# One prologue folded into the attention part: one input norm, inputs rounded tile by tile, a first step that begins with the context

## The chip, the cores and the metric

The kernel runs on one NeuronCore of a Trainium2 chip. The metric is the device time of one execution in microseconds. The engines are TensorE (PE: matmuls, with PEld its weight loads), VectorE (DVE), ScalarE (ACT), GpSimd (POOL) and SyncE (SP), which issues most DMAs. They run beside each other and wait for one another on semaphores.

## What is computed

A gated transformer block with cross attention and a mixture of experts on `x` of 8 sequences of 112 tokens and 512 channels. Cut to what matters here:

```
h   = layernorm(layernorm(x)) * ln_w + ln_b                 # two norms in a row, eps 1e-5
xq_n = fp8(bf16(clip(h / in_scale_n, -448, 448)))           # n = q, qx, k, v: four roundings
q, qx, k, v = xq_n @ (wq, wqx, wk, wv)                      # then a layernorm per head of 128
kx, vx      = split(ctx @ w_kv_x)                           # ctx of 375 rows, not rounded
core, xout  = attention(q, k, v), attention(qx, kx, vx)     # 16 heads, 8 groups
x = x + tanh(g_x) * (fp8(concat(core, xout) / smooth) @ wproj) * scale
x = x + tanh(g_f) * experts(layernorm(x))                   # 8 experts, 2 of them per token
```

Two norms in a row are one: with mean m and variance v of a token, the second norm of the first is (x - m) / sqrt(v(1 + e) + e*e).

## The kernel before

Three parts stand behind each other, each with its own block of instruction streams, and a barrier between them.

`quantise_inputs` is the prologue. The 896 tokens are 7 tiles of 128. VectorE takes the statistics of a tile, GpSimd makes root and shift (L303, L305), ScalarE applies them (L314), and this twice for every tile, the second norm three tiles behind the first. TensorE transposes (L347), ScalarE applies `ln_w` and `ln_b` into `hT` (L320) and makes, for each of the four input scales, a bf16 copy of all 4 x 896 columns (L330). VectorE rounds each copy to fp8 in five operations of 3584 columns (`round_fp8`, L410 to L414) into `xq`. Between these copies ScalarE centres the first group's weights (`centre`, L149 to L154: 128 columns at a time are scaled, and the mean of the head's columns, made by VectorE at L130, is added).

`attention` does the heads in 4 groups (`gp`), each with its own 2048 columns of weights, and in a group a step per sequence (8). A matmul in f32 is done as three products of split operands: `w_hi` and `w_lo` are the high and low part of the weights, `c_hi` and `c_lo` of the context. ScalarE writes the high parts, VectorE or GpSimd the low ones. `xqs` is the tile of `xq` converted for the matmul (`inputs`, L1049). In a step `project(s, j)` makes six products: j = 0, 1, 2 from tokens (queries, cross queries, keys and values), j = 3, 4, 5 from the three thirds of the context. Steps 0 to 6 of a group have a token tile; step 7 has none left and only the rest. While step s is projected, step t = s - 1 has its scores, softmax and outputs: TensorE's, VectorE's and ScalarE's orders are written out by hand in `step`. The very first step (change = "first") has no t beside it. It needs all of `xq`, all `w_hi` and `w_lo`, and does j = 0 to 5 in that order.

In the first four steps with a tile behind the first one VectorE also takes the means of the next group's weights (`weights.means`), and ScalarE centres them one step later.

`projected_experts` follows and isn't touched.

The numbers `pj_no` and `st_no` give the count that the semaphores of projections and statistics have reached at product j of a step.

Of the kernel before, what the change touches and what calls it, by code (L numbers as in the profile page):

```python
# [19 lines left out]
U16 = mybir.dt.uint16  # L20
# [40 lines left out]
def transformer_block(nc, x, ctxT, vecs, scalars, smooth, w_in, wproj, Wr, Wg, Wu, Wd, out):  # L61
# [3 lines left out]
    with ExitStack() as top:  # L65
# [24 lines left out]
        with ExitStack() as c:  # L90
            xq = sb(c, "xq", [P, 4, KB, NT], BF16)
            smi = sb(c, "smi", [P, GP, 8])
            wsc = sb(c, "wsc", [P, 4, KB])
            wmul = sb(c, "wmul", [P, KB, LNC // HD])
            weights = CentredWeights(c, sb, sem, w_in, shared, wsc, wmul)
            with ExitStack() as c0:
                quantise_inputs(nc, c0, sb, ps, sem, x, vecs, scalars, smooth, vec, scal, gate,
                                proj_scale, ident, mhalf, epst, xq, smi, weights)
            with ExitStack() as c1:
                attention(nc, c1, sb, ps, sem, ctxT, wproj, cat_w, vec, ident, mhalf, epst, xq, smi,  # L100
                          weights, shared, wp_load, cat_load, results)
# [5 lines left out]
class CentredWeights:  # L107
# [3 lines left out]
    def __init__(self, c, sb, sem, w_in, shared, wsc, wmul):  # L111
# [3 lines left out]
        self.in_done = sem(c, "w_in_done")  # L115
# [5 lines left out]
    def fetch(self, sp, g, k):  # L121
        sp.dma_start(self.raw[:, k, :], self.w_in[g, :, k, :]).then_inc(self.in_done, 16)

    def means(self, v, g, k):

        mean = self.mean[:, bass.ds(k, 1), :].rearrange("p a b -> p (a b)")
        v.wait_ge(self.in_done, 16 * KB * (g + 1))
# [103 lines left out]
def quantise_inputs(nc, c, sb, ps, sem, x, vecs, scalars, smooth, vec, scal, gate, proj_scale,  # L231
                    ident, mhalf, epst, xq, smi, weights):

    LAG = 3
    NORMS = []
    for j in range(TJ + LAG):
        if j < TJ:  # L240
            NORMS.append((0, j))
        if j >= LAG:
            NORMS.append((1, j - LAG))
    N = len(NORMS)
    wsc, wmul = weights.wsc, weights.wmul

    xs = sb(c, "xs", [P, TJ, D])
    st = sb(c, "st", [P, N, 6])
    mv = sb(c, "mv", [P, N, 2])
    rstd = sb(c, "rstd", [P, N])  # L250
    shift = sb(c, "shift0", [P, N])
    hT = sb(c, "hT", [P, KB, NT])
    inv = sb(c, "inv", [P, 4, KB])
    smr = sb(c, "smr", [P, GP, 8])
    yq = sb(c, "yq", [P, 2, KB, NT], BF16)
    ye = sb(c, "ye", [P, KB, NT], BF16)
    ysum = sb(c, "ysum", [P, KB, NT], BF16)
    pt = ps(c, "pt", [P, 4, 512])

    vec_in = sem(c, "vec_in")  # L260
    x_in = [sem(c, f"x_in{j}") for j in range(TJ)]
    const_done = sem(c, "const_done")
    pool_self = sem(c, "pool_self")
    bn_done = sem(c, "bn_done0")
    ag_done = sem(c, "ag_done0")
    stat_done = sem(c, "stat_done")
    rstd_pow = sem(c, "rstd_pow0")
    rstd_done = sem(c, "rstd_done")
    normed = sem(c, "normed")
    dve = sem(c, "dve_chain0")  # L270
    tr_done = sem(c, "tr_done")
    hT_done = sem(c, "hT_done")
    scal_done = sem(c, "scal_done")
    inv_done = sem(c, "inv_done")
    y_done = sem(c, "y_done")
    round_done = sem(c, "round_done")
    block = c.enter_context(nc.Block())

    @block.sync
    def _(sp):  # L280
        tokens = x.rearrange("b t d -> (b t) d")
        sp.dma_start(xs[:, 0, :], tokens[0:P, :]).then_inc(x_in[0], 16)
        sp.dma_start(vec[:, :], vecs).then_inc(vec_in, 16)
        sp.dma_start(scal[:, :], scalars.partition_broadcast(P)).then_inc(vec_in, 16)
        sp.dma_start(smr[:, :, :], smooth).then_inc(vec_in, 16)
        for j in range(1, TJ):
# [1680 lines left out]
```

## Time and profile before

| | us |
|---|---|
| median of three timed runs (1179.20 to 1185.28) | 1180.48 |
| the profiled execution | 1179.41 |
| its span | 1177.6 |
| TensorE busy | 1081.8 (92%) |
| VectorE busy | 808.2 (69%) |
| ScalarE busy | 726.1 (62%) |
| GpSimd busy | 500.3 (42%) |
| mean granted TensorE clock | 0.967 of full speed |

Shares are means over stages that differ: the prologue, the attention and the experts. What a change in one stage is worth is read from that stage. Busy shares of TensorE count pipelined matmuls and are no measure of its peak.

### The profile page before, as it was taken

How to read it: one execution, taken by the hardware profiler on the slowest of the kernel's cores; microseconds unless marked ns; L12 is line 12 of the kernel's file. 1: busy time of each engine (PE TensorE's matmuls, PEld its weight loads, DVE VectorE, ACT ScalarE, POOL GpSimd, SP SyncE). 2: the span in 40 equal slices, each digit the busy share in tenths (PEclk: the TensorE clock that was granted, in tenths of full speed). 3: DMA queues.
4: the chain of work that ended last, by engine and by line, in shares of the span. 5: the costliest groups of instructions: out<-in, count | busy, mean ns of one | idle time of the engine just before them, and what ended most of it. 6: DMA issues, size and time to landing. Idle time of an engine off the chain costs nothing. (4 is left out here: it accounts for less than half of the span.)

```text
span 1177.6 us, 19559 instructions
## 1 busy us (share of the span) xinstructions
PE 1081.8 (92%) x5662; PEld 890.0 (76%) x5662; DVE 808.2 (69%) x1626; ACT 726.1 (62%) x2082; POOL 500.3 (42%) x587
## 2 busy tenths in 40 slices
PE   1079999999999999999999999998999959999996
PEld 1058888878888887888878888886888747777885
DVE  7967887797878787878789677767545776565000
ACT  7967887865788876687875676565231323333442
POOL 3065454445454544554545445542000125565432
PEclk9589999999999999999999999999999969999999
DMA  5032111115111113211111411110955237674220
GB/s 206 0 135 104 43 44 35 36 60 186 35 51 44 44 35 137 101 44 35 51 52 36 140 52 37 42 43 10 342 187 194 104 129 217 193 228 120 49 45 0
DMA packets 51714, 107.38 MB, mean 91 GB/s; under 512 B 5984, under 2 KB 26464, under 8 KB 49568
## 3 DMA queue, kind: packets, MB, share of 16 engines
q1 hardware_dynamic: 46912, 97.00, 25.2%
q0 software_dynamic: 4704, 9.18, 3.4%
q8 instruction: 49, 0.80, 0.3%
q14 instruction: 49, 0.40, 0.1%
HBM read 91.48 MB, written 16.52 MB: 92 GB/s over the span
## 5 line engine op out<-in xcount | busy, mean ns | idle before, releaser
L632 POOL TENSOR_TENSOR rs<-va,mhalf 125x2 f32<-125x2 f32 (+1 forms) x180 | 201.3, 1118 | 14.1
L638 POOL TENSOR_TENSOR c_lo<-c_raw,c_hi 128x500 fp32r<-128x500 f32 x96 | 122.8, 1279 | 183.3 <-ACT c_hi L689 183.3
L848 PE MATMUL p_proj<-w_hi,xqs 128*128 128x512 f32 (+2 forms) x464 | 157.0, 358 | 42.8 <-DVE w_lo L567 41.0
L875 PE MATMUL p_proj<-w_hi,c_hi 128*125 128x512 f32 x384 | 165.4, 431 | 0.0
L875 PE MATMUL p_proj<-w_hi,c_lo 128*125 128x512 f32 x384 | 151.5, 395 | 0.0
L875 PE MATMUL p_proj<-w_lo,c_hi 128*125 128x512 f32 x384 | 151.3, 394 | 0.0
L848 PE MATMUL p_proj<-w_lo,xqs 128*128 128x512 f32 (+2 forms) x464 | 147.9, 339 | 0.0
L848 PEld LDWEIGHTS p_proj<-w_hi,xqs 128*128 128x128 f32 (+1 forms) x464 | 86.4, 186 | 51.4 <-issue 43.5
L625 POOL TENSOR_TENSOR va<-ss,epst 125x2 f32<-125x2 f32 (+1 forms) x180 | 47.2, 262 | 170.7 <-DVE ss L1057 101.1
L767 ACT ACTIVATE pcross<-p_cross,nmax 112x375 f32<-112x375 f32 x128 | 73.6, 585 | 43.5 <-DVE nmax L1086 43.4
L919 PE MATMUL p_cross<-kxT,qxT 128*112 128x375 f32 x256 | 97.0, 480 | 0.0
L848 PEld LDWEIGHTS p_proj<-w_lo,xqs 128*128 128x128 f32 (+1 forms) x464 | 86.7, 187 | 8.3
L875 PEld LDWEIGHTS p_proj<-w_hi,c_hi 128*125 128x125 f32 x384 | 71.3, 186 | 18.4 <-issue 0.2
L875 PEld LDWEIGHTS p_proj<-w_lo,c_hi 128*125 128x125 f32 x384 | 71.3, 186 | 17.9
L875 PEld LDWEIGHTS p_proj<-w_hi,c_lo 128*125 128x125 f32 x384 | 71.1, 185 | 18.0
L729 ACT ACTIVATE nkx<-p_proj 125x256 f32<-125x256 f32 x96 | 38.4, 400 | 63.5 <-PE p_proj L875 63.5
L950 PE MATMUL p_out<-pcrossT,valx 125*128 125x224 f32 x354 | 76.6, 352 | 0.0
L1093 DVE TENSOR_SCALAR pcross<-pcross,linv 112x375 f32<-112x375 f32 x128 | 72.0, 562 | 4.6
L1086 DVE TENSOR_REDUCE nmax<-p_cross 112x1 f32<-112x375 f32 x128 | 69.0, 543 | 2.9 <-PE p_cross L919 0.2
L1469 POOL DMA_INDIRECT out<-p_cat,of_row x21 | 45.9, 2186 | 57.9 <-ACT p_cat L1570 50.2
L950 PEld LDWEIGHTS p_out<-pcrossT,valx 125*128 125x128 f32 x354 | 66.8, 189 | 0.3
L933 PEld LDWEIGHTS p_tr<-ident,pcross 112*125 112x125 f32 x384 | 51.9, 188 | 17.7 <-issue 13.5
(268 smaller groups left out, 2857.1 us busy)
## 6 DMA issues: line engine op xcount, KB each, us to landing
c_raw<-in_ctxT SPq DMA_DIRECT2D x96, 250.0 KB, 2.6
shared<-in_w_in SPq DMA_DIRECT2D x16, 1024.0 KB, 8.9
shared<-in_wproj SPq DMA_DIRECT2D x32, 256.0 KB, 3.9
raw_g<-in_Wg SPq DMA_DIRECT2D x8, 1024.0 KB
raw_u<-in_Wu SPq DMA_DIRECT2D x8, 1024.0 KB, 6.2
raw_d<-in_Wd SPq DMA_DIRECT2D x8, 1024.0 KB, 5.5
cat_scratch<-results SPq DMA_DIRECT2D x32, 224.0 KB, 2.0
shared<-cat_scratch SPq DMA_DIRECT2D x2, 1792.0 KB, 9.2
```

Of the source, the lines that this page charges most:

```text
L625: pool.tensor_tensor(va[0:rows, lo:hi], ss[0:rows, lo:hi], epst[0:rows, lo:hi], ALU.add).then_inc(va_done, 1)
L632: pool.tensor_tensor(rs[0:rows, lo:hi], va[0:rows, lo:hi], mhalf[0:rows, lo:hi], ALU.pow).then_inc(rs_done, 1)
L638: pool.tensor_tensor(flat(c_lo[:, k, :, :]), flat(c_raw[:, k, :, :]), flat(c_hi[:, k, :, :]).bitcast(F32), ALU.subtract).then_inc(cl_done, 1)
L767: act.activation(pcross[0:T, h, :], p_cross[0:T, h % 2, 0:TC], ACT.Exp, bias=nmax[0:T, 4 + h:5 + h], accum_out=lsum[0:T, 4 + h:5 + h]).the ...
L848: m = pe.matmul(out, xqs[:, n, k, 0:rows], (w_hi, w_lo)[i % 2][:, k, lo:lo + w], start=(i == 0), stop=(i == 2 * KB - 1))
L875: m = pe.matmul(bank[0:CT, :], a[:, ch, k, :], w[:, k, CKX:CV], start=(i == 0), stop=(i == 3 * KB - 1))
L919: pe.matmul(p_cross[0:T, h % 2, 0:TC], qxT[:, t[1] % 2, h, :], kxT[:, h // HPG, :], start=True, stop=True).then_inc(sx_rdy, 1)
L933: m = pe.transpose(p_tr[0:CT, 1 - h % 2, k * T:(k + 1) * T], pcross[0:T, h, k * CT:(k + 1) * CT], ident[0:T, 0:T])
L950: m = pe.matmul(out[:, HPG * T:2 * HPG * T], valx[0:CT, par, k, g * P:(g + 1) * P], flat(pcrossT[0:CT, k, HPG * g:HPG * (g + 1), :]), star ...
L1086: v.tensor_reduce(nmax[0:T, 4 + h:5 + h], p_cross[0:T, h % 2, 0:TC], AX, ALU.max, negate=True).then_inc(mx_done, 1)
L1093: v.tensor_scalar(pcross[0:T, h, :], pcross[0:T, h, :], linv[0:T, 4 + h:5 + h], None, ALU.mult).then_inc(nx_done, 1)
L1469: pool.indirect_dma_start(out=tokens[:, :], out_offset=bass.IndirectOffsetOnAxis(ap=of_row[:, 1, i:i + 1], axis=0), in_=y[:, i % 2, :], in ...
```

## The change

Prologue and attention are one part with one block. There is one norm per tile. The transposes of all seven tiles go to one memory of all eight PSUM banks (`pt`), of which `p_proj`, `p_tr`, `p_self`, `p_cross` and `p_out` are now views, and ScalarE reads them there: `scaled_inputs(k)` writes, for one block of 128 channels, the four scaled copies of all 896 tokens straight into `xq`. `hT` and the two sets of bf16 copies are gone. `xq` is rounded in place by `rounding(u, half, first, last)`: one tile of 128 tokens, half of its channels, all four copies, five operations of 1024 columns, and `first` to `last` says which of them. Tiles 0, 1 and 2 are rounded in the first step, tiles 3 to 6 in pieces in steps 1 to 4 of the first group.

The first step does the context products (j = 3, 4, 5) first. Their weight columns come in a DMA of their own, ahead of the context and the other columns, and are centred by VectorE (`other_columns`). The other columns of channel block 0 are scaled and centred by GpSimd, those of blocks 1 to 3 by VectorE (`own_columns`), where ScalarE did all of it. All five groups of `w_lo` of the first step are VectorE's; GpSimd had two (L567). The token tiles share the memory `work` with `pcross`, `valx` and `pcrossT`; `sqx` has one buffer for three.

```diff
-            pool.tensor_tensor(rstd[:, one], mv[:, i, 1:2], mhalf[:, 0:1], ALU.pow).then_inc(rstd_pow, 1)
...
+            v.tensor_scalar(mv[:, j, 1:2], mv[:, j, 1:2], 1.0 + EPS, EPS * EPS, ALU.mult,
+                            ALU.add).then_inc(stat_done, 1)
...
+def turn_of(pos, j):
+
+    return (j + 3) % 6 if pos == FIRST else j
...
+    def own_columns(eng, k):
+
+        eng.wait_ge(weights.mu, k + 1)
+        for h in range(CKX // HD):
+            cols = w_raw[:, k, h * HD:(h + 1) * HD]
+            n = 0 if h < CQX // HD else 1 if h < CK // HD else 2
+            eng.tensor_scalar(cols, cols, weights.wsc[:, n, k:k + 1], weights.mean[:, k, h:h + 1], ALU.mult, ALU.add)
+        cols = w_raw[:, k, CV:WC]
+        eng.tensor_scalar(cols, cols, weights.wsc[:, 3, k:k + 1], None, ALU.mult).then_inc(w_cen, 1)
...
+        sp.dma_start(w_raw[:, :, CKX:CV], weights.w_in[0, :, :, CKX:CV]).then_inc(wx_in, 16)
+        for k in range(NC):
+            load_c(0, 0, k)
+        for k in range(KB):
+            sp.dma_start(w_raw[:, k, 0:CKX], weights.w_in[0, :, k, 0:CKX]).then_inc(weights.in_done[k], 16)
+            sp.dma_start(w_raw[:, k, CV:WC], weights.w_in[0, :, k, CV:WC]).then_inc(weights.in_done[k], 16)
...
             if change == "first":
-                for n in range(len(USED)):
+                scaled_inputs(0)
+                w_high(g, 4, change)
+                for j in range(3):
+                    c_high(s, j)
+                for j in range(3):
+                    scaled_inputs(j + 1)
+                    take(s, j + 3)
+                for n in range(4):
                     w_high(g, n, change)
                 for j in range(3):
-                    c_high(s, j)
-                for j in range(6):
                     take(s, j)
...
-            pe.wait_ge(pj_done, pj_no(s, j) - 2)
+            pe.wait_ge(pj_done, pj_no(s, j) - (1 if j == 0 and s == (0, 1) else 2))
...
+            if s == FIRST and j == 3:
+                pe.wait_ge(y_done, 1)
...
+        def rounding(u, half, first, last):
+
+            y = xq[:, :, 2 * half:2 * half + 2, u * P:(u + 1) * P]
+            e = re[:, :, :, :]
+            v.wait_ge(y_done, 2 * half + 2)
+            for n in range(first, last + 1):
+                v.wait_ge(rq, 10 * u + 5 * half + n)
+                if n == 0:
+                    ins = v.tensor_scalar(y, y, FP8_MAX, -FP8_MAX, ALU.min, ALU.max)
+                elif n == 1:
+                    ins = v.tensor_scalar(e.bitcast(U16), y.bitcast(U16), 0x7F80, None, ALU.bitwise_and)
+                elif n == 2:
+                    ins = v.tensor_scalar(e, e, 2.0 ** -6, 1.5 * 2.0 ** 4, ALU.max, ALU.mult)
+                else:
+                    ins = v.tensor_tensor(y, y, e, (ALU.add, ALU.subtract)[n - 3])
+                ins.then_inc(rq, 1)
...
+            spread = s is not None and s[0] == 0 and 1 <= s[1] < TJ - 2
             if A: sums(s, 0)
+            if spread: rounding(s[1] + 2, 0, 0, 2)
...
+            if spread: rounding(s[1] + 2, 0, 3, 3)
             if Q: take_self(t)
...
             if A: scale(s, 1)
+            if spread: rounding(s[1] + 2, 0, 4, 4)
             if A: scale(s, 2)
...
             if A: scale(s, 3)
+            if spread: rounding(s[1] + 2, 1, 0, 1)
             if Q: smoothed(t, 1)
...
             if A: scale(s, 5)
+            if spread: rounding(s[1] + 2, 1, 2, 4)
...
             if change == "first":
-                w_low(g, 0)
-                w_low(g, 1)
                 w_low(g, 4)
+                for j in range(1, KB):
+                    own_means(j)
+                for j in range(1, KB):
+                    own_columns(v, j)
+                rounding(0, 0, 0, 4)
+                rounding(0, 1, 0, 4)
+                inputs(s)
+                for n in range(4):
+                    w_low(g, n)
                 smooth_of(g)
-                for j in range(6):
-                    if j < 3:
-                        sums(s, j)
-                    if j > 0:
-                        scale(s, j - 1)
-                    if j == 3:
-                        inputs((s[0], s[1] + 1))
-                scale(s, 5)
-
-        inputs(FIRST)
+                for j in range(3, 6):
+                    scale(s, j)
+                rounding(1, 0, 0, 4)
+                rounding(1, 1, 0, 4)
+                for j in range(3):
+                    sums(s, j)
+                inputs((s[0], s[1] + 1))
+                for j in range(3):
+                    scale(s, j)
+                rounding(2, 0, 0, 4)
+                rounding(2, 1, 0, 4)
```

The order of instructions, first on VectorE from the last rounding of the prologue into the first step, as before (`ye`, `ysum` and `yq` are the old bf16 copies; `shared` is the raw weights):

```order
L414 TENSOR_TENSOR xq<-ysum,ye 128x3584
L96 UNCONDITIONAL_BRANCH
L1014 UNCONDITIONAL_BRANCH
L1049 CAST xqs<-xq 128x512 x3
L1050 CAST xqs<-xq 128x4x112
L567 TENSOR_TENSOR w_lo<-shared,w_hi 128x4x512 x3
L1027 COPY smg<-smi 128x8
L1057 TENSOR_REDUCE ss<-sq 128x4 x2
```

And on VectorE in the changed kernel from its first `w_lo` to the `w_lo` of the queries (`re` is the new exponent buffer):

```order
L432 TENSOR_TENSOR w_lo<-shared,w_hi 128x4x512
L1030 TENSOR_REDUCE w_mean<-shared 128x10
L1033 TENSOR_TENSOR w_mean<-w_mean,wmul 128x10
L426 TENSOR_SCALAR shared<-shared,wsc,w_mean 128x128 x10
L428 TENSOR_SCALAR shared<-shared,wsc 128x256
L1043 TENSOR_SCALAR xq<-xq 128x4x2x128
L1045 TENSOR_SCALAR re<-xq 128x1024
L1047 TENSOR_SCALAR re<-re 128x1024
L1049 TENSOR_TENSOR xq<-xq,re 128x4x2x128 x2
L1060 CAST xqs<-xq 128x512 x3
L1061 CAST xqs<-xq 128x4x112
L432 TENSOR_TENSOR w_lo<-shared,w_hi 128x4x512 x2
```

(The rows of L1030 to L1033 and of L426 to L428 stand three times each there, those of L1043 to L1049 twice; they are shown once.) Means, columns and one tile's rounding now stand between the context's `w_lo` and the queries' `w_lo`.

VectorE in a step of the first group, before, from the scaling of the first two cross probabilities to the sums of the cross queries:

```order
L1091 RECIPROCAL linv<-lsum 112x1
L1093 TENSOR_SCALAR pcross<-pcross,linv 112x375
L1099 COPY pselfT<-p_tr 112x448
L1057 TENSOR_REDUCE ss<-sq 128x4
L1104 COPY pcrossT<-p_tr 125x3x112
```

And the same place in the changed kernel (`work` holds `pcross` and `pcrossT`, `bank` is PSUM):

```order
L1102 RECIPROCAL linv<-lsum 112x1
L1104 TENSOR_SCALAR work<-work,linv 112x375
L1049 TENSOR_TENSOR xq<-xq,re 128x4x2x128
L1110 COPY pselfT<-bank 112x448
L1068 TENSOR_REDUCE ss<-sq 128x4
L1115 COPY work<-bank 125x3x112
```

One of a half's five roundings now stands ahead of the copy of `pselfT`.

ScalarE's first step in the changed kernel, from the first `scaled_inputs` to the second take of the context (L665 is `scaled_inputs`, `nkx` the keys of the context):

```order
L665 ACTIVATE xq<-bank,xof,xsc 128x896 x4
L575 ACTIVATE w_hi<-shared 128x4x512
L580 ACTIVATE c_hi<-c_raw 128x500 x3
L665 ACTIVATE xq<-bank,xof,xsc 128x896 x4
L621 ACTIVATE nkx<-bank 125x256
L622 ACTIVATE work<-bank 125x256
L597 ACTIVATE sqx,ss<-bank 125x128 x2
L665 ACTIVATE xq<-bank,xof,xsc 128x896 x4
```

The scaling of the inputs is now split in four and stands around the takes of the context.

## Rows read from the trace of the kernel before

**Rows 1.** The page, busy time and share of the span of TensorE and others.

```profile
PE 1081.8 (92%) x5662; PEld 890.0 (76%) x5662; DVE 808.2 (69%) x1626; ACT 726.1 (62%) x2082; POOL 500.3 (42%) x587
```

**Rows 2.** By stage: start:end, length, each engine's busy us, PEclk, DMA share, GB/s.

```profile
24.80:64.80 40.00, 0.02 (x1) 0.05 (x1) 36.28 (x30) 39.35 (x73) 0.00 (x0) 0.50 0.06 19
64.80:83.40 18.60, 16.78 (x69) 13.21 (x69) 14.59 (x14) 9.86 (x25) 17.87 (x15) 0.88 0.22 60
...
107.20:202.60 95.40, 95.40 (x531) 79.95 (x529) 76.21 (x168) 79.39 (x260) 47.23 (x60) 1.00 0.15 43
```

**Rows 3.** Waits from 0 to 110 us: total, times, longest.

```profile
PE p_proj L848 <- DVE w_lo L567: 41.0, 1, 41.0
```

**Rows 4.** Groups by line and shape, 0 to 60 us: busy us, mean ns.

```profile
L330 ACT ACTIVATE yq<-hT,inv 128x896 bf16<-128x896 f32 x16 | 15.2, 1032 | 0.0
L413 DVE TENSOR_TENSOR ysum<-yq,ye 128x3584 bf16<-128x3584 bf16 x4 | 8.1, 2026 | 0.1
L412 DVE TENSOR_SCALAR ye<-ye 128x3584 bf16<-128x3584 bf16 x4 | 4.4, 1094 | 0.1
L381 DVE TENSOR_SCALAR wsc<-vec,scal 128x4 f32<-128x4 f32 x4 | 0.6, 224 | 0.0
```

**Rows 5.** VectorE in time, prologue and first step: start, us, idle before.

```profile
5.68 0.69 DVE L373 BATCH_NORM_STATS2 st<-xs 128x6 f32<-128x512 f32 x1 [1.37 <-DMA xs<-in_x]
...
60.73 1.10 DVE L1049 CAST xqs<-xq 128x512 fp32r<-128x512 bf16 x3 [1.83 <-PEq L835]
...
62.34 4.49 DVE L567 TENSOR_TENSOR w_lo<-shared,w_hi 128x2048 fp32r<-128x2048 f32 x2 [0.21 <-ACT w_hi L684]
```

**Rows 6.** ScalarE in time, first step.

```profile
60.40 7.41 ACT L684 ACTIVATE w_hi<-shared 128x2048 fp32r<-128x2048 f32 x5 [0.62 <-PEq L96]
67.71 1.62 ACT L689 ACTIVATE c_hi<-c_raw 128x500 fp32r<-128x500 f32 x3
...
77.88 0.38 ACT L729 ACTIVATE nkx<-p_proj 125x256 f32<-125x256 f32 x1 [2.13 <-PE p_proj L875]
...
78.83 0.22 ACT L705 ACTIVATION_READ_ACCUMULATOR sqx<-p_proj 125x1 f32 x1
```

**Rows 7.** TensorE in time: first step's second and third matmul, second step's first.

```profile
65.34 0.63 PE L848 MATMUL p_proj<-w_lo,xqs 128*128 128x512 f32 x1
65.77 0.63 PE L848 MATMUL p_proj<-w_hi,xqs 128*128 128x512 f32 x1
...
83.39 0.47 PE L848 MATMUL p_proj<-w_hi,xqs 128*128 128x512 f32 x1
```

**Rows 8.** VectorE in time in the third step: its four pauses, two bf16 operations.

```profile
115.32 0.62 DVE L1072 TENSOR_REDUCE nmax<-p_self 112x4 f32<-112x448 f32 x1 [1.58 <-PE p_self L912]
...
120.08 0.62 DVE L1099 COPY pselfT<-p_tr 112x448 f32<-112x448 f32 x1 [0.73 <-PE p_tr L926]
...
126.80 0.42 DVE L1066 TENSOR_TENSOR nk<-nk,rs 128x256 f32<-128x256 f32 x1 [0.59 <-POOL rs L632]
...
131.34 0.62 DVE L1111 TENSOR_TENSOR results<-p_out,smg 128x448 bf16<-128x448 f32 x1 [1.11 <-PE p_out L950]
...
134.42 0.39 DVE L202 TENSOR_SCALAR results<-results 128x896 bf16<-128x896 bf16 x1
...
135.70 0.63 DVE L212 TENSOR_TENSOR results<-results 128x896 bf16<-128x896 bf16 x1
```

**Rows 9.** VectorE and TensorE in time in the second step, at the bank of `pselfT`.

```profile
96.26 0.62 DVE L1099 COPY pselfT<-p_tr 112x448 f32<-112x448 f32 x1 [0.74 <-PE p_tr L926]
...
97.03 0.55 PE L933 MATMUL p_tr<-ident,pcross 112*125 112x112 f32 x3
```

**Rows 10.** GpSimd and VectorE in time in the second step.

```profile
99.78 1.27 POOL L638 TENSOR_TENSOR c_lo<-c_raw,c_hi 128x500 fp32r<-128x500 f32 x1
...
100.25 1.02 DVE L1093 TENSOR_SCALAR pcross<-pcross,linv 112x375 f32<-112x375 f32 x1
...
101.37 0.42 DVE L1093 TENSOR_SCALAR pcross<-pcross,linv 112x375 f32<-112x375 f32 x1
```

More of the change, by code:

```diff
@@ L114, in __init__ @@
         self.mean = sb(c, "w_mean", [P, KB, LNC // HD])
-        self.in_done = sem(c, "w_in_done")
+        self.in_done = [sem(c, f"w_in_done{k}") for k in range(KB)]
         self.seen = sem(c, "w_seen")
@@ L589, in _ @@
             for b in range(2):
-                for k in range(NC):
+                for k in range(NC if s0 + b > 0 else 0):
                     load_c(s0 + b, b, k)
@@ L670, in _ @@
     def _(act):
+        act.sem_inc(weights.cen, 4)
         act.sem_inc(ch_done, 3)
@@ L681, in w_high @@
                 act.wait_ge(pj_rdy, pj_no((g - 1, u), j))
-            act.wait_ge(w_cen, 4 * (g + 2))
+            if change == "first" and n == 4:
+                act.wait_ge(wx_cen, 1)
+            else:
+                act.wait_ge(w_cen, 4 * (g + 2))
             lo, hi = USED[n]
@@ L768, in exp_cross, with scaled_inputs @@
                            bias=nmax[0:T, 4 + h:5 + h], accum_out=lsum[0:T, 4 + h:5 + h]).then_inc(ex_done, 1)
+        def scaled_inputs(k):
+            for n in range(4):
+                last = act.activation(xq[:, n, k, :], pt[:, k, 0:NT], ACT.Identity, bias=xof[:, n, k:k + 1],
+                                      scale=xsc[:, n, k:k + 1])
+            last.then_inc(y_done, 1)
         def last_step(s, t, g, change):
@@ L983, in step @@
                 return last_step(s, t)
-            if change not in ("first", "new"):
+            if change == "first":
+                for j in (3, 4, 5, 0, 1, 2):
+                    project(s, j, g)
+                return
+            if change != "new":
                 g = None
@@ L1010, in step @@
             if Q: outputs(t, 1)
+        pe.wait_ge(const_done, 1)
+        for j in range(TJ):
+            pe.wait_ge(normed, j + 1)
+            for k in range(KB):
+                m = pe.transpose(pt[:, k, j * P:(j + 1) * P], xs[:, j, k * P:(k + 1) * P], ident[:, :])
+            m.then_inc(tr_done, 1)
         passes(pe, step)
@@ new lines, in other_columns @@
+        def other_columns():
+            heads = w_raw[:, :, CKX:CKX + 2 * HD].rearrange("p k (h d) -> p k h d", d=HD)
+            mean = weights.mean[:, :, CKX // HD:CKX // HD + 2]
+            v.wait_ge(wx_in, 16)
+            link(v.tensor_reduce(mean, heads, AX, ALU.add))
+            link(v.tensor_scalar(mean, mean, -1.0 / HD, None, ALU.mult))
+            for k in range(KB):
+                for h in range(CKX // HD, CKX // HD + 2):
+                    cols = w_raw[:, k, h * HD:(h + 1) * HD]
+                    last = v.tensor_scalar(cols, cols, weights.mean[:, k, h:h + 1], None, ALU.add)
+            last.then_inc(wx_cen, 1)
```

327 lines of the change are left out of this document (141 added, 186 removed).

## The prediction, on record before the changed kernel ran

> **What bounds the kernel.** I read the busy table first: TensorE is busy 92% of the span [rows 1], so time can come only from work taken off TensorE or from the stretches in which it stands still. The table by stage shows where these are. From 24.8 to 64.8 us TensorE does nothing (0.02 us busy), VectorE and ScalarE are full (36.3 and 39.4 of 40 us), and its granted clock is at the lower of its two levels. Later, from 107.2 to 202.6 us, it is busy throughout [rows 2]. The list of waits names the end of the gap: 41.0 us of waiting for `w_lo`, made by VectorE [rows 3]. So the input norm, the rounding of all inputs and the centring of the weights are a prologue of 64.8 us, and the first step, which ends at 83.4 us, is filled badly. The change touches only these, and the four steps that now carry rounding. Everything behind should move as a block. What is gained is how much earlier the second step begins, less what the next steps lose.
>
> **The norm.** Fourteen rounds of statistics become seven. The second round starts at 5.68 us, when its data are there [rows 5], and a round takes 0.69 us for the statistics plus three tiny operations behind each other, about 1.06 us together: the last ends near 12.0 us. GpSimd's root and shift, ScalarE's normalising and four transposes of that tile bring me to 15.0 us (an estimate).
>
> **ScalarE's new chain.** Each `scaled_inputs(k)` is four operations of 128x896. The nearest row is L330 with 1.03 us (16 of them), of which some 0.95 go by before the next starts [rows 4]; source and bias differ, so I allow 0.9 to 1.1. Four are 3.8 us. A quarter of `w_hi` (2048 of 8192 columns in 7.41 us) is 1.85 us, the three `c_hi` 1.62 us, and to take one third of the context in costs 1.1 us, from its first row to its last [rows 6]. So: 15.0 + 3.8 = 18.8, `w_hi` for the context columns 20.7, `c_hi` 22.3, second `scaled_inputs` 26.1.
>
> **First context product.** VectorE's half of the context weights, `w_lo`, is 4.49 / 2 = 2.25 us [rows 5]: ready at 23. TensorE starts at 23 instead of 64.8 us, cold: in the old trace the first matmuls ran at the lower clock after such a gap [rows 2, 7]. The first third takes 5.1 us that way (twelve matmuls 0.43 us apart, as cold there [rows 7]), the others 2.8 each at the higher clock; thirds end near 28.2, 31.0 and 33.8. ScalarE goes on: take 29.3, scale 33.1, take 34.2, scale 38.0, take 39.1, `w_hi` of the query columns 41.0.
>
> **VectorE, the chain that now decides.** From 23 us: three means of 1280 columns (at the 1.1 ns a column of `w_lo` [rows 5] 1.4 us, with the small product behind it 1.63) 4.9 us, to 28. Then `own_columns` for three blocks, 30 operations of 128 columns with two scalar operands and three of 256. No row shows this shape. From below: 0.14 each, as 512 columns are converted in 1.10 / 3 us [rows 5]. From above: 0.31, since an operation with one scalar operand and only four columns already shows 0.22 [rows 4]. Blocks cost 1.6 to 3.4 us, and I take 2.7, near the second row: end at 36. GpSimd does the fourth block beside it, from 26 us on; even at three times VectorE's price (8 us) it is done before 39 us, when ScalarE first needs all four.
>
> A rounding of half a tile is five operations of 1024 bf16. The steps of before show the same five at 896 columns, 0.39 and 0.63 us [rows 8], the prologue at 3584, 1.09 and 2.03 us [rows 4]. Interpolated, with some 0.04 us to the next: 3 x 0.46 + 2 x 0.73 = 2.8 us, 5.65 a tile. Tile 0: first half to 39.0, second to 41.8. That second half waits for ScalarE's fourth scaling (38.0 by the list above), an added wait with little slack: behind it on VectorE stand `inputs` and all `w_lo` of the queries, for which TensorE waits; if ScalarE is a microsecond later than I count, all that follows is. `inputs` 1.4: 43.2. `w_lo` for the other four groups, 6144 columns, 6.7: 50. TensorE runs behind it and ends the first step near 53. Scaling three thirds 1.3, tile 1 5.65, three sums 1.6, `inputs` 1.4: 60. So **the second step starts at about 60 us instead of 83.4 [rows 7], a lead of 23.4**. TensorE has stood still for 7 us again; about 4.4 us then run at half speed (a mean clock of 0.88 over 18.6 us says so of the old start [rows 2]) and cost 2. VectorE in the same time does three scalings (1.7), tile 2 (5.65), a sum and the first rounding piece, and comes to its first maximum at about 70, before 91.5: the same lead within 0.5. **Lead after that: 21.**
>
> **What the steps give back.** A step before is 23.8 us (`pselfT` at 96.26 and at 120.08 [rows 8, 9]), TensorE full. VectorE's pauses in it are 1.58, 0.73, 0.59 and 1.11 us [rows 8], 4.0 in sum, plus 0.3 that only waits for ScalarE. Rounding adds 5.65 to each of four steps. The pieces are laid into the pauses: 1.4 before the maximum, 0.73 before `pselfT`, 0.73 before `nk`, 0.9 before the second `results`. Only the last piece, 1.9 us, stands where there was no pause, and it shares 1.58 with the first piece of the next step. So VectorE is 1.9 + 1.4 - 1.6 = 1.7 us late at the maximum in steps 2, 3 and 4. How much lateness TensorE forgives is seen at `pselfT`: VectorE ends it at 96.88, and the transposes that need the bank begin at 97.03 [rows 9]. The slack is 0.15 us, so TensorE loses 1.5 us a step, 4.5 in three.
>
> To that comes contention. While GpSimd's `c_lo` ran, from 99.78 to 101.05, VectorE's scaling of `pcross` took 1.02 us instead of the usual 0.42 [rows 10]: it did not end before GpSimd's instruction had. The rounding has three operations a half of this one-input kind, and where one meets a `c_lo` (three a step) it may lose up to 1.2 us. The pieces mostly lie where GpSimd does roots, so I take 0.3 a step, 1 in all. The Trainium skill says of this in "GPSIMD Engine Reference" (section 1, Specifications) that the two engines share their SBUF interfaces, and that VectorE's two-port modes and its instructions with two SBUF inputs are those that contend. By that rule all five operations of a rounding are exposed; the trace agrees for the one-input case (1.02 against 0.42 us).
>
> **The sum.** 21 - 4.5 - 1 = 15.5 us. The profiled execution took 1179.41 us (span 1177.6), so 1163.9; the median of the three timed runs is 1.07 above it, so **1164.5 us** for the median. The rest costs nothing that I can find: the single `sqx` buffer adds a wait of ScalarE for its own earlier instruction, long over; the separate `in_done` semaphores only release earlier; the `work` tile shares memory between things that do not live together. On SyncE's queue 1.05 MB of context columns and 0.75 MB of context stand ahead of the weights; at the rate of the first load this delays the last block to about 20 us, and VectorE asks for it at 26. The next group's weights are fetched after the first step as before, thus earlier by the lead.
>
> **Rivals.** (1) The roundings hide almost wholly: TensorE's lead over VectorE at the first maximum takes up the lateness, or the pieces are shorter than interpolated. For it: the 4.0 us of pauses. Against: 5.65 is more than 4.0, and the slack is 0.15. It would leave 20 to 21: 1159. (2) The steps saturate: each piece meets `c_lo`, and roots that GpSimd is late with delay `nk`; VectorE then loses 3 us in each of four steps, and the weight columns take their upper price (2 us). 21 - 12 - 2 = 7: 1173. For it is the 1.02 us row; against it, that `c_lo` is only three times 1.3 us in 23.8.
>
> (3) Slower: the rounding no longer runs at the old rate, since it now reads `xq` in rows of 128 columns with gaps, four by two of them, where both old roundings read one run. If its two-input operations run at the rate of f32 (2048 columns of `w_lo` in 2.25 us, so 1024 in 1.13) and the others at that of the conversions (512 in 0.37, so 1024 in 0.7) [rows 5], a half costs 2 x 1.13 + 3 x 0.7 = 4.3 us with the gaps between, a tile 8.6 instead of 5.65. Three tiles ahead of the second step and four in the steps, 7 x 3 = 21 us, more than the lead that is left: 1185. It decides from 2.2 us a tile on (15.5 / 7). Against it: the conversions of `xq` read just such rows, and still take only 0.37 us for 512, a third less than f32 would at `w_lo`'s rate (0.56) [rows 5]. The Trainium skill, "VectorE: DVE Perf Modes" (What auto-detection actually checks), makes the fast modes depend on 16-bit types, unit step, SBUF and an even outermost dimension; by that rule the gaps do not matter, and the sum stays at 5.65 a tile. No row here shows a four-dimensional bf16 operation.
>
> (4) The first step starts early but nothing is gained because the weights still decide: its price is in the chain above (product on the queries at 45 instead of 64.8), and a part of it is in (2).
>
> **Numbers.** Forecast (lead 12 to 19) 0.55; (1) 0.17; (2) 0.20; (3) 0.06; anything else slower or equal 0.02. The range of 8 in 10: 1157 to 1173. A difference under 0.5% (5.9 us) can hardly be told from none: faster by more than that 0.88 (case (2) gives a fifth of its chance to "within"), within 0.06, slower 0.06.
>
> **What would show it.** In the changed profile: TensorE's first context matmul near 23 us and a second gap near 34 to 45; the second step's first product near 60; fourteen halves of five 1024-column operations at 0.42 and 0.70 us; steps 2 to 4 of the first group at 25 to 26 us with VectorE without a pause, and from step 6 on 23.8 again. Wrong would be: a second step later than 64; a bf16 piece above 0.9 us; a step of the first group above 27; or any step after the first group changed in length.

## The result, and the profile after

The changed kernel took 1166.73 us (median of four runs, 1166.17 to 1168.32), the kernel before 1181.12: the ratio is 0.988, 95% interval 0.986 to 0.990. That is 14.4 us less; forecast were 16.0 (1164.5 us), and the range of 1157 to 1173 held it. The profiled execution took 1166.94 us (span 1164.7). The sum under the forecast was less right than its total, as the traces show, and a part of the agreement was luck.

First the prologue and the first step, VectorE in time (start, us, operation, idle before and what ended it). They answer to [rows 5].

```profile
13.29 1.22 DVE L1000 TENSOR_REDUCE w_mean<-shared 128x8 f32<-128x1024 f32 x1 [0.28 <-DMA shared<-in_w_in]
...
21.47 2.29 DVE L432 TENSOR_TENSOR w_lo<-shared,w_hi 128x2048 fp32r<-128x2048 f32 x1 [1.42 <-ACT w_hi L575]
...
29.44 3.77 DVE L426 TENSOR_SCALAR shared<-shared,wsc,w_mean 128x128 f32<-128x128 f32 x10
...
33.39 2.65 DVE L426 TENSOR_SCALAR shared<-shared,wsc,w_mean 128x128 f32<-128x128 f32 x10
...
39.05 0.42 DVE L1043 TENSOR_SCALAR xq<-xq 128x1024 bf16<-128x1024 bf16 x1
...
40.42 1.42 DVE L1049 TENSOR_TENSOR xq<-xq,re 128x1024 bf16<-128x1024 bf16 x2
...
46.10 6.76 DVE L432 TENSOR_TENSOR w_lo<-shared,w_hi 128x2048 fp32r<-128x2048 f32 x4
```

The chain is the one forecast, with the operations at the forecast prices (0.42 to 0.43 and 0.71 us for a rounding's operations, 6.76 for the four `w_lo`), but 3 us late at the first rounding. TensorE's pauses in the same trace, answering to [rows 3, 7]:

```profile
25.01 0.76 PE L789 MATMUL bank<-w_hi,c_hi 128*125 128x512 f32 x1 [9.54 <-POOL c_lo L527]
48.53 0.76 PE L760 MATMUL bank<-w_hi,xqs 128*128 128x512 f32 x1 [13.09 <-DVE w_lo L432]
62.53 0.77 PE L760 MATMUL bank<-w_hi,xqs 128*128 128x512 f32 x1 [6.08 <-DVE xqs L1061]
...
102.29 0.59 PE L840 MATMUL bank<-ident,pself 112*112 112x112 f32 x4 [1.24 <-DVE pself L1091]
103.17 0.55 PE L847 MATMUL bank<-ident,work 112*125 112x112 f32 x3 [0.29 <-ACT kxT L635]
104.56 0.55 PE L847 MATMUL bank<-ident,work 112*125 112x112 f32 x3 [0.20 <-DVE pselfT L1110]
```

The second step starts at 62.5 us, 20.9 earlier than before (23.4 forecast). In the third step (and the next two, which repeat these rows) TensorE now waits for VectorE's `pself`, where it had waited for nothing, and then, by shorter waits, for ScalarE's `kxT` and VectorE's `pselfT`. The starts of the first score matmuls of each step show where the lead goes (columns: start, duration, eight matmuls each):

```profile
71.58 0.94 PE L826 MATMUL bank<-kT,qT 128*112 128x112 f32 x8
95.73 0.94 PE L826 MATMUL bank<-kT,qT 128*112 128x112 f32 x8
121.89 0.94 PE L826 MATMUL bank<-kT,qT 128*112 128x112 f32 x8
147.99 0.95 PE L826 MATMUL bank<-kT,qT 128*112 128x112 f32 x8
174.07 0.95 PE L826 MATMUL bank<-kT,qT 128*112 128x112 f32 x8
198.53 0.94 PE L826 MATMUL bank<-kT,qT 128*112 128x112 f32 x8
...
407.88 0.95 PE L826 MATMUL bank<-kT,qT 128*112 128x112 f32 x8
```

The same matmuls of the kernel before, for comparison:

```profile
90.51 0.95 PE L912 MATMUL p_self<-kT,qT 128*112 128x112 f32 x8
114.33 0.94 PE L912 MATMUL p_self<-kT,qT 128*112 128x112 f32 x8
...
209.70 0.95 PE L912 MATMUL p_self<-kT,qT 128*112 128x112 f32 x8
...
419.03 0.95 PE L912 MATMUL p_self<-kT,qT 128*112 128x112 f32 x8
```

The lead, by which a matmul starts earlier than the same one before, is 18.9 us at the first score, and 11.2 at the sixth and still at the fifteenth (198.53 against 209.70, 407.88 against 419.03). In between three intervals are 26.1 us instead of 23.8, and the ones beside them 24.15 and 24.5. So the steps took back 7.8 us; forecast were 5.5. And yet the span fell by 12.9, not by 11.2. The 1.7 us more lie at the start of the experts. One row by stage of each kernel, same place, 20 us (columns as in [rows 2]); of before, and after:

```profile
812.00:832.00 20.00, 15.85 (x67) 12.36 (x68) 16.41 (x36) 6.03 (x16) 4.67 (x16) 0.91 0.45 156
```

```profile
801.00:821.00 20.00, 16.06 (x75) 12.72 (x76) 16.42 (x36) 5.37 (x14) 4.67 (x16) 1.00 0.44 155
```

TensorE's mean granted clock is 0.91 before and 1.00 after: some 3.4 us at the lower level (1.2 GHz in place of 2.4) in one execution, none in the other. The last experiment takes that up.

VectorE loses time in a long step at two places. The first is its end. VectorE, then GpSimd in time, then the VectorE operation of before that answers to the second row ([rows 8] has the one ahead of it):

```profile
95.27 0.63 DVE L208 TENSOR_TENSOR results<-results 128x896 bf16<-128x896 bf16 x1
95.93 1.56 DVE L211 TENSOR_TENSOR results<-results 128x896 bf16<-128x896 bf16 x1
...
99.26 0.62 DVE L1083 TENSOR_REDUCE nmax<-bank 112x4 f32<-112x448 f32 x1
```

```profile
95.39 1.61 POOL L527 TENSOR_TENSOR c_lo<-c_raw,c_hi 128x500 fp32r<-128x500 f32 x1 [5.62 <-ACT c_hi L580]
```

```profile
136.36 0.62 DVE L215 TENSOR_TENSOR results<-results 128x896 bf16<-128x896 bf16 x1
```

The same bf16 operation that took 0.62 us before takes 1.56, in the four steps in which the late VectorE runs it beside GpSimd's `c_lo`. The maximum starts 3.5 us behind the scores (99.26 against 95.73), where it was 1.0 (91.49 against 90.51): VectorE is 2.5 us late, not 1.7.

The second place is the pause ahead of `nk` (0.59 us before, [rows 8]). A piece of the rounding was laid into it, but the pause is still there behind the piece. VectorE, then GpSimd in the changed kernel, then GpSimd before:

```profile
109.83 0.69 DVE L1049 TENSOR_TENSOR xq<-xq,re 128x1024 bf16<-128x1024 bf16 x1
111.11 0.43 DVE L1077 TENSOR_TENSOR nk<-nk,rs 128x256 f32<-128x256 f32 x1 [0.59 <-POOL rs L521]
```

```profile
108.93 2.15 POOL L521 TENSOR_TENSOR rs<-va,mhalf 128x2 f32<-128x2 f32 x1
```

```profile
125.22 1.54 POOL L632 TENSOR_TENSOR rs<-va,mhalf 128x2 f32<-128x2 f32 x1
```

GpSimd's root, for which `nk` waits, takes 2.15 us instead of 1.54 in the steps in which VectorE runs that piece beside it; in the step without a piece it is 1.55 again (185.61), and so it is in the kernel without any rounding in the steps (106.07, 1.54 us). So this pause takes up none of the work.

### The profile page after: what moved, and what is told of

It is laid out like the page before. It is cut to its first block and busy times, and to the rows that moved or that the text cites. A ratio compares the mean times of both kernels' runs of the same rounds, so it can differ in the third digit from the quotient of the medians.

```text
span 1164.7 us, 19668 instructions
## 1 busy us (share of the span) xinstructions
PE 1087.5 (93%) x5662; PEld 891.7 (77%) x5662; DVE 820.7 (70%) x1695; ACT 697.9 (60%) x2015; POOL 498.9 (43%) x582
## 5 line engine op out<-in xcount | busy, mean ns | idle before, releaser
L760 PE MATMUL bank<-w_hi,xqs 128*128 128x512 f32 (+2 forms) x464 | 157.8, 360 | 19.2 <-DVE w_lo L432 13.1
L789 PE MATMUL bank<-w_hi,c_hi 128*125 128x512 f32 x384 | 166.3, 433 | 9.5 <-POOL c_lo L527 9.5
L789 PE MATMUL bank<-w_hi,c_lo 128*125 128x512 f32 x384 | 152.1, 396 | 0.0
L789 PE MATMUL bank<-w_lo,c_hi 128*125 128x512 f32 x384 | 151.7, 395 | 0.0
L760 PE MATMUL bank<-w_lo,xqs 128*128 128x512 f32 (+2 forms) x464 | 148.7, 341 | 0.0
L760 PEld LDWEIGHTS bank<-w_hi,xqs 128*128 128x128 f32 (+1 forms) x464 | 87.0, 187 | 27.7 <-issue 19.7
L659 ACT ACTIVATE work<-bank,nmax 112x375 f32<-112x375 f32 x128 | 73.6, 585 | 41.7 <-DVE nmax L1097 41.5
L833 PE MATMUL bank<-kxT,qxT 128*112 128x375 f32 x256 | 96.9, 480 | 0.0
L760 PEld LDWEIGHTS bank<-w_lo,xqs 128*128 128x128 f32 (+1 forms) x464 | 87.1, 188 | 8.4
L789 PEld LDWEIGHTS bank<-w_hi,c_hi 128*125 128x125 f32 x384 | 71.8, 187 | 27.9 <-issue 9.9
L864 PE MATMUL bank<-work 125*128 125x224 f32 x384 | 83.1, 352 | 0.0
```

The lines of the kernel that those rows point to most:

```text
L659: act.activation(pcross[0:T, h, :], p_cross[0:T, h % 2, 0:TC], ACT.Exp, bias=nmax[0:T, 4 + h:5 + h], accum_out=lsum[0:T, 4 + h:5 + h]).the ...
L760: m = pe.matmul(out, xqs[:, n, k, 0:rows], (w_hi, w_lo)[i % 2][:, k, lo:lo + w], start=(i == 0), stop=(i == 2 * KB - 1))
L789: m = pe.matmul(bank[0:CT, :], a[:, ch, k, :], w[:, k, CKX:CV], start=(i == 0), stop=(i == 3 * KB - 1))
L833: pe.matmul(p_cross[0:T, h % 2, 0:TC], qxT[:, t[1] % 2, h, :], kxT[:, h // HPG, :], start=True, stop=True).then_inc(sx_rdy, 1)
L864: m = pe.matmul(out[:, HPG * T:2 * HPG * T], valx[0:CT, par, k, g * P:(g + 1) * P], flat(pcrossT[0:CT, k, HPG * g:HPG * (g + 1), :]), star ...
```

## The experiments

All kernels are edits of the changed kernel. Medians are of four or five runs (ten for the third). The changed kernel itself had a median of 1166.73 us at one time and 1168.54 at another, so differences of a microsecond or two between edits are read from the starts in the traces and not from the medians. "Interval" is the time from one step's first score to the next one's, 23.8 us before and 26.1 in the changed kernel's long steps.

### Without the rounding in the steps

```diff
-            spread = s is not None and s[0] == 0 and 1 <= s[1] < TJ - 2
+            spread = False
...
-            if s[0] == 0 and has_tile(s):
+            if s[0] == 0 and u < 3:
                 v.wait_ge(rq, 10 * (u + 1))
```

> The changed kernel, with the rounding of token tiles 3 to 6 left out (their scaled inputs stay unrounded); all else is as it was. Theory A (the rounding pieces saturate VectorE in steps 1 to 4 of the first group and delay TensorE by 2.3 us in each of steps 2, 3 and 4, and by 0.3 and 0.6 beside them, 7.8 us in all): scores of the first attention stay near 71.6 us or come 0.6 earlier, the four intervals between scores are 23.8 us each, and the time is 7 to 8 us below the changed kernel, about 1159. Rival B (the steps are longer for something else that the change brought, the one sqx buffer, the shared memory or the semaphores): the intervals stay above 25.5 us and the time within 2 us of 1166.7.

1160.41 us (ratio to before 0.982, interval 0.980 to 0.984). First score at 71.35, the next at 95.19, 119.02, 142.85, 166.69: every interval is 23.8. At the fifteenth score the lead is 19.3 us (399.75), 8.1 more than the changed kernel's. The time is 6.3 us less, not 8; its trace has a slow clock stretch of its own just ahead of the experts (794 to 798 us). Theory A holds: all that the steps lose hangs on the rounding, and the other changes cost them nothing.

### A short `c_lo`

```diff
-            pool.tensor_tensor(flat(c_lo[:, k, :, :]), flat(c_raw[:, k, :, :]),
-                               flat(c_hi[:, k, :, :]).bitcast(F32), ALU.subtract).then_inc(cl_done, 1)
+            n = 4 if k == 0 and s[0] == 0 and 1 <= s[1] < TJ - 1 else KB * CT
+            pool.tensor_tensor(flat(c_lo[:, k, :, :])[:, 0:n], flat(c_raw[:, k, :, :])[:, 0:n],
+                               flat(c_hi[:, k, :, :]).bitcast(F32)[:, 0:n], ALU.subtract).then_inc(cl_done, 1)
```

> The changed kernel, in which GpSimd's c_lo of the first context third writes only 4 of its 500 columns in steps 1 to 5 of the first group. Theory A1 (of the 2.3 us a step, 0.9 come from VectorE's two-input operation on the results meeting this c_lo, 1.56 us in place of 0.63): that operation is back at 0.63, the three long intervals fall from 26.1 to 25.2 us, the whole gains 2.5 to 3 us. Rival (the operation is slow for another reason, or TensorE's delay is set elsewhere): it stays above 1.2 us, or the intervals stay at 26.1.

1163.81 us. The operation on the results, VectorE in time:

```profile
94.92 0.63 DVE L208 TENSOR_TENSOR results<-results 128x896 bf16<-128x896 bf16 x1
95.58 0.62 DVE L211 TENSOR_TENSOR results<-results 128x896 bf16<-128x896 bf16 x1
```

It is back at 0.62, the intervals are 25.2 (95.38, 120.61, 145.75, 170.97). So 0.9 of the 2.3 us a step are the meeting of these two operations. The other 1.4 come with VectorE's load, and with them the pause ahead of `nk` that stays, 0.59 us in this trace too.

### All rounding ahead of the steps

```diff
+            spread = False
...
-                rounding(2, 0, 0, 4)
-                rounding(2, 1, 0, 4)
+                for u in range(2, TJ):
+                    rounding(u, 0, 0, 4)
+                    rounding(u, 1, 0, 4)
```

> The changed kernel, with tiles 3 to 6 rounded at the end of the first step instead of in pieces in the steps behind it. Same work. By theory A the steps go back to 23.8 us (7.8 us won) and the first maximum comes later by four tiles less the first piece, 4 x 5.8 - 1.4 = 22 us: the time is 13 to 15 us above the changed kernel, about 1181, the level of before. If the pauses of VectorE in the steps were worth nothing, it would be as fast as the changed kernel.

1183.62 us, 0.27% slower than before (ratio 1.003, interval 1.0015 to 1.004), and 16.9 above the changed kernel, 2 to 4 more than expected (by its starts it is 14.7 us behind at the fifteenth score, 422.55, which is within the expectation). TensorE waits 20.6 us for `pself` in one place (releaser in the trace), and then all intervals are 23.8. The same four tiles cost 7.8 us in pieces and some 22.7 in a block (the one long interval is 46.56 us): the steps take up two thirds of the work. It also says that without the spreading the whole change would not have been faster.

### Token products first

```diff
-    return (j + 3) % 6 if pos == FIRST else j
+    return j
...
-                for j in (3, 4, 5, 0, 1, 2):
+                for j in range(6):
                     project(s, j, g)
```

with ScalarE taking j = 0 to 5 behind all `w_high`, and VectorE's sums between the two halves of tile 1, its scalings behind `inputs`.

> The changed kernel, with TensorE's and ScalarE's order of the first step as before: token products first, then the context. VectorE's order is kept but for the sums of the first step, which stand between two roundings. Theory C (what starts the second step is VectorE's chain, which ends at 62 us, and TensorE has 13 us of pause in the first step): TensorE's first product comes near 48, its first step ends near 61 with 5 us of cold clock, and the time is within 2 us of the changed kernel. Rival D (beginning with the context is what the gain rests on): the second step starts 6 to 10 us later and the time is 1173 to 1177.

1172.11 us: neither. The first product comes at 47.6 and the first score at 70.39, even earlier than with the context first (71.58), so rival D is wrong about the place: the second step does not start 6 us later. The loss comes behind it. Intervals are 27.95, 25.88, 27.78 and 27.53. TensorE's mean clock by stage, three stretches of 10 us in this kernel:

```profile
75.00:85.00 10.00, 7.86 (x31) 5.38 (x30) 9.09 (x23) 6.83 (x27) 5.72 (x7) 0.83 0.10 26
128.00:138.00 10.00, 8.27 (x31) 5.59 (x30) 9.22 (x23) 8.29 (x31) 5.74 (x7) 0.83 0.20 53
155.00:165.00 10.00, 8.50 (x33) 5.82 (x32) 9.21 (x23) 7.75 (x30) 5.74 (x7) 0.83 0.23 60
```

Each holds some 3.4 us at half speed; TensorE had stood for 1.85 us ahead of the first (77.56, waiting for `pself`) and for 1.0 to 1.2 ahead of the others. VectorE reached its first maximum 1.4 us later than in the changed kernel (74.53 against 73.14), having the context's scalings still before it. I ran the same kernel again to see whether that is chance.

> The kernel with the token products first, unaltered, once more. Its first trace began its first attention no later than the changed kernel (70.4 against 71.6 us) and still took 5.4 us longer; it showed three stretches of 3.4 us at half speed in steps 1 to 4, where the changed kernel had none. If these belong to its slightly longer pauses, they are there again and the median is 1170 to 1174; if they were chance, the trace has one or none and the median is 1167 to 1169.

1172.57 us, and the slow stretches are there again after the first and the third pause, not after the fourth; the first interval is again 27.9. The first may belong to this kernel: both traces have it, behind a pause of 1.85 us where the changed kernel's longest is 0.19 (78.45). For the third that isn't shown, as its pause (1.24 and 1.19 us) is no longer than the changed kernel's (1.24, 1.20, 1.22). So beginning with the context is worth 4 to 5 us, and what the traces show as its way is not TensorE's earlier start. One part is VectorE's work done before the steps, which removes the pause of 1.85 us; the other is the slow stretches, in the first trace 1.7 and 1.45 us in the third and fourth interval against the changed kernel's. How much of that other part belongs to the order and how much to chance was not separated.

### Three edits that should win time back

`c_hi` of the first context third earlier on ScalarE:

```diff
             if change == "new": w_high(g, 4, change)
+            if A: c_high(s, 0)
             if Qt: turned(t, 0)
             if A: take(s, 0)
             if Qt: turned(t, 1)
             if Qt: turned(t, 2)
-            if A: c_high(s, 0)
```

> The changed kernel, with ScalarE's c_hi of the first context third at the head of each step with a token tile (ahead of the turned queries, in ScalarE's pause of 2.4 us) in place of behind them. GpSimd's c_lo then runs some 5 us earlier, beside VectorE's reduction of the weight means, which reads one input. Theory A1: VectorE's last operation on the results is back at 0.63 us, the three long intervals between scores fall from 26.1 to 25.2 us, and the time falls by 2 to 3 us against the changed kernel (1164 to 1165). Rival: the early c_lo meets another operation of VectorE and costs the same there; intervals stay at 26 and the time within 1 us.

1164.00 us. Intervals 25.2 (95.06, 120.18, 145.40, 170.60), the lead at the fifteenth score 15.2 us (403.82) for 11.2. As expected, and with the full work; the lead grows by 4.1 us, 2.8 of it in the three long intervals and the rest beside them. `c_lo` now starts at 89.04, beside the reduction of the means, which keeps its 1.75 us.

```profile
89.29 1.75 DVE L126 TENSOR_REDUCE w_mean<-shared 128x12 f32<-128x1536 f32 x1
...
95.22 0.62 DVE L211 TENSOR_TENSOR results<-results 128x896 bf16<-128x896 bf16 x1
```

The scaling of the keys later on VectorE:

```diff
-            if A: scale(s, 2)
             if A and Q: smoothed(t, 0)
...
             if A: inputs((s[0], s[1] + 1))
+            if A: scale(s, 2)
```

> The changed kernel, with VectorE's scaling of the keys (nk) behind the conversion of the next inputs, so that it no longer waits 0.59 us for GpSimd's root in front of them. Where VectorE is the bound (steps 2 to 4) each step should be 0.5 to 0.6 us shorter, 1.5 to 1.8 us in all; the other steps stay at 23.8. If TensorE's delay does not hang on VectorE's total but on the pieces ahead of the maximum alone, the intervals stay at 26.1.

1167.19 us; intervals 25.9 instead of 26.1, less than half of what was expected. VectorE no longer waits for the root, but comes to the next `results` early and waits there for TensorE:

```profile
139.90 0.62 DVE L1122 TENSOR_TENSOR results<-bank,smg 128x448 bf16<-128x448 f32 x1 [0.36 <-PE bank L864]
```

Of the 0.59 us 0.36 are lost again there. The lead is 12.8 us, 1.7 more than in the first trace (0.7 of it in the three intervals), but the time shows nothing of it; this trace has the slow stretch at the experts. Inconclusive in time, small by structure.

Two weight blocks on GpSimd, and the last scaling ahead of the second take:

```diff
                 own_columns(pool, 0)
+                own_columns(pool, 1)
...
-                for j in range(3):
-                    scaled_inputs(j + 1)
-                    take(s, j + 3)
+                scaled_inputs(1)
+                take(s, 3)
+                scaled_inputs(2)
+                scaled_inputs(3)
+                take(s, 4)
+                take(s, 5)
...
-                for j in range(1, KB):
+                for j in range(2, KB):
                     own_columns(v, j)
```

> The changed kernel, with two changes in its first step: GpSimd scales and centres the weight columns of blocks 0 and 1 (before: 0 alone), VectorE of 2 and 3; ScalarE makes the last scaled_inputs before it takes the second context third. If VectorE's chain decides when the second step starts, that comes 2.0 to 3.0 us earlier (59.5 to 60.5 in place of 62.5) and the time falls by the same. Against it: GpSimd's operations hold up VectorE's, as in the first block now (3.77 us in place of 2.65), which would leave 1 us or less.

1165.60 us. The second step starts at 59.81 (62.53 in the changed kernel), as expected: VectorE's chain decides. (Two things were changed at once; which of them was needed is not shown.) The first score is at 68.94, but the interval behind the second is 27.8: a slow clock stretch lies in it (mean clock 0.83 from 99 to 109 us), and two more at the experts (0.83 from 799 to 819), where the changed kernel's first trace had none. Of the 2.7 us won, 1.1 are left in the median, and the profiled execution (1167.74 us) shows none of them.

All three together:

> The three edits of the other kernels of this call together (c_hi early, nk late, two blocks on GpSimd). If each takes away a part of its own, the sum is 6 to 7.5 us against the changed kernel, 1159 to 1161; if TensorE's slack at pselfT absorbs a part, 4 to 6 us.

1161.74 us, 18.1 below before (ratio 0.983, 0.980 to 0.987) and 5 below the changed kernel's first median (6.8 below its second). The intervals are 24.9 (93.40, 118.33, 143.26, 168.19). By structure the lead grew by 6.4, as expected; a slow stretch at the experts is in the trace. It is the fastest kernel here that does all the work.

And with the roundings split around the maxima:

```diff
-            if spread: rounding(s[1] + 2, 0, 0, 2)
+            if spread: rounding(s[1] + 2, 0, 0, 0)
...
             if Q: max_cross(t, 1)
+            if spread: rounding(s[1] + 2, 0, 1, 2)
```

> The kernel with all three edits, and in steps 1 to 4 the second and third of a half's five roundings behind the maxima, where VectorE pauses 0.6 us for ScalarE's exponentials, instead of ahead of them. VectorE's lateness is what lengthens the steps (theory A), so the maximum comes 0.9 us earlier and the normalising 0.3 later for it: intervals between scores 24.9 to 24.3 us, the second to fourth together 1.5 to 2 us; time 1159 to 1161. If the lateness at the normalising alone counts, nothing is won.

1162.65 us: nothing won, the intervals are 25.07. The expectation forgot GpSimd once more. VectorE, then GpSimd in time:

```profile
96.42 0.42 DVE L1049 TENSOR_SCALAR re<-xq 128x1024 uint16<-128x1024 uint16 x1
96.87 1.38 DVE L1051 TENSOR_SCALAR re<-re 128x1024 bf16<-128x1024 bf16 x1
98.17 0.17 DVE L1093 RECIPROCAL linv<-lsum 112x4 f32<-112x4 f32 x1
```

```profile
96.17 1.79 POOL L527 TENSOR_TENSOR c_lo<-c_raw,c_hi 128x500 fp32r<-128x500 f32 x1
```

The second `c_lo` of the step runs there, and the rounding that fell into it took 1.38 us instead of 0.43, all that the split had won.

### The changed kernel again

> The changed kernel unaltered, on another chip job. TensorE's structure of starts should be that of the first profile within 1 us (second step at 62 to 63, three intervals at 26.1). Open is whether the half-speed stretch of 3.4 us at the start of the experts, which the kernel before had and the changed one had not, belongs to the kernel or falls as it may: if it is the kernel's, the trace shows none again and the median is 1166 to 1167.5; if not, it may show one, 1.7 us longer.

1168.54 us (four runs, ratio to before 0.989, 0.987 to 0.991). The second step starts at 62.02, the three intervals are 27.3, 25.9 and 26.2, the lead at the fifteenth score is 10.7 (408.30). By stage:

```profile
802.00:822.00 20.00, 16.62 (x71) 12.96 (x72) 16.19 (x36) 5.32 (x12) 4.68 (x16) 0.91 0.45 156
98.00:110.00 12.00, 10.50 (x43) 7.67 (x42) 11.06 (x26) 9.23 (x36) 7.74 (x7) 0.86 0.28 73
```

The slow stretch at the experts is there now, and one more in the third step. So neither belongs to a kernel: the same code has them or not, each is some 3.4 us long and costs about 1.7 us, and the first trace of the changed kernel was a lucky one. All thirteen traces of this document have the same pause of 2.4 us at the start of the experts; behind it seven have the slow stretch and six have not. That is a part of the spread of 2 to 6 us between single runs of one kernel, but not all of it: of the four runs here the fastest (1165.76 us) and the slowest (1170.92) both show a mean clock of 0.975. What makes the rest is open.

## Why the prediction was right, point by point

**What bounds, and where.** Right. TensorE was idle to 64.8 us for VectorE's work, the gain is an earlier second step, and behind the first group only the slow clock stretch at the experts changed a length.

**The context products** started at 25.0, not 23. I named `w_lo` as the last to come; it was GpSimd's `c_lo`, for which the sum had no term, and three of which took 5.28 us beside VectorE instead of 3 x 1.27. It cost nothing, since TensorE waited 13.1 us afterwards.

**VectorE's chain** ran as said, 39.05 at the first rounding instead of 36. Of the 3 us one is the first block of columns, 3.77 us beside GpSimd's block instead of 2.65; the others, at 2.83 with their value columns, were near the 2.7 taken. The rest is the start, as the chain's first `w_lo` ended 0.8 us later than said, and small products of the means held up by `c_lo` (0.91 us for 0.17). Second step 62.5 for 60, lead at the scores 18.9 for 21.

**The steps** are the term that was mis-sized: 4.5 + 1 = 5.5 forecast, 7.8 measured. The mechanism was right: at `pselfT` nearly all lateness goes through (2.3 us late, 2.3 lost), and the pieces of the rounding cost what was interpolated. But the 0.15 us read there as slack are hardly any. Where TensorE does wait for `pselfT` in the changed kernel, it starts 0.14 us behind the copy as well (104.42 and 104.56), so this is the handover, and by that the 1.7 us of lateness would have cost 1.7 a step and not 1.5. The longest wait in the step, 1.24 us for `pself`, I had not named; what sets the total is `pselfT`, behind which the transposes start 8.83 us after the scores instead of 6.53. What I left small was the contention, 0.3 us a step; the short `c_lo` and the early `c_hi` both show 0.9 at one operation, and GpSimd's longer root kept the pause at `nk`, which I had counted as filled, open by 0.6 more. I looked for it at the new operations and at one-input ones. It fell on an old two-input operation that had been clear of `c_lo` by 0.9 us and was moved into it by the lateness. The rule cited from the Trainium skill's "GPSIMD Engine Reference" (section 1), that instructions with two SBUF inputs contend as well, is thus borne out here for an operation that is nothing but such (1.56 against 0.62 us), and I had weighed it with the one-input row alone.

**The clock.** The sum had no term for slow stretches behind the first step. By structure the forecast lead of 15.5 was 11.2, 4.3 too many, and below the 12 to 19 that I had called the forecast; the first trace got 1.7 back from a slow stretch that was absent. That part of the agreement is luck: in its second measurement the same kernel was 12.2 us below its own before, not 14.4. The range held both medians, and the truth lies nearer to rival (2) than the forecast says: the steps did saturate.

**The rivals.** (1) is out, as the first experiment shows: the rounding in the steps costs 8 us. Of (2) the mechanism was there at some 2.3 us a step. (3), slower modes of the rounding in rows with gaps, is out: 0.42 and 0.71 us for 1024 columns, the rates of the contiguous rows. (4) is out: the product on the queries starts at 48.53 us, later than the 45 forecast, but far ahead of 64.8.

**The signs of being wrong.** One came true in the first trace: a piece of the rounding took 1.50 us (limit 0.9), in the second step at 71.27 us, beside a `c_lo` (71.23, 1.26 us). Another came in the second trace, a step of 27.3 us (limit 27), with a slow clock stretch in it. And VectorE in the long steps is not without a pause: 0.61 us for ScalarE's exponentials and the 0.59 at `nk` are left.

## What to carry to other kernels

When work is laid into the pauses of an engine, add up its whole step: 4.0 us of pauses do not hold 5.65, less so when a pause that waits for another engine stays behind the new work (0.59 us at `nk`), and what is left over passes undiminished to the bounding engine where that takes the result as soon as it is there. Then move every old instruction of that engine by the lateness, and look what runs on GpSimd there: an operation that was clear of it by a microsecond no longer is. Moving GpSimd's `c_lo` away, by one moved line of ScalarE's, was a cheap cure (2.7 us in the median, 4.1 by the starts), and a kernel's single trace should be checked for stretches of slow TensorE clock before its time is explained.

## What the runs showed of the hardware

- A GpSimd two-input subtraction of 128x500 and a VectorE operation on two inputs of 128x896 bf16 slow each other: 1.61 and 1.56 us beside each other, 1.26 and 0.62 apart. A reduction on VectorE beside it keeps its 1.75 us. One-input bf16 operations of 1024 columns went from 0.43 to 1.38 and 1.50 us beside it.
- A root of 128x2 on GpSimd took 1.54 us in the kernel before and 2.15 beside VectorE's added two-input bf16 operation of 1024 columns.
- bf16 operations on four by two rows of 128 with gaps run at the rate of one run of columns.
- TensorE's clock fell to its lower level for some 3.4 us in some executions of the same code and not in others, after pauses of 1 to 2.4 us, in the steps and around the start of the experts. Behind the pause of 2.4 us that all kernels share it did so in seven of thirteen traces. The kernel with a pause of 1.85 us in its second step had it there in both traces.
- Between the end of VectorE's copy of `pselfT` and TensorE's next transposes lie 0.14 us where TensorE waited for it (104.42 to 104.56), and 0.15 in the kernel before, where it did not (96.88 to 97.03).
